# A 176-wide expert product without its zero padding: 48 rows in place of 128

## The reference

```python
def _L1_ffn_ref(hidden_states, gate_weight, w_gate, w_up, w_down):
    x = hidden_states.reshape(-1, H)              # 1024 tokens, H = 256
    scores = jax.nn.softmax(x @ gate_weight.T)    # E = 28 experts
    topk_w, topk_idx = jax.lax.top_k(scores, 6)
    topk_w = topk_w / (topk_w.sum(axis=-1, keepdims=True) + 1e-20)
    cw = ...                                      # 1024 x 28, zero but for the six
    def step(y, inp):
        wg, wu, wd, w_tok = inp                   # 256x176, 256x176, 176x256
        h = jax.nn.silu(x @ wg) * (x @ wu)
        return (y + w_tok[:, None] * (h @ wd), None)
```

## Time and profile before

| | us |
|---|---|
| median of 3 runs | 969.02 |
| the runs | 969.22, 964.23, 969.02 |
| profiled execution | 969.22 |
| its span, first to last instruction | 967.4 |
| mean granted TensorE clock | 0.828 |

### The profile page before, as it was taken

How to read it: one execution, slowest core, us unless ns; L and a number is a source line. 1 busy time by engine, 2 the same in 40 slices (tenths; PEclk the granted TensorE clock), 3 DMA queues, 4 the chain that set the end, 5 groups by cost and what they waited for, 6 DMA issues and landing times. The chain is left out here.

```text
span 967.4 us, 13065 instructions
## 1 busy us (share of the span) xinstructions
PE 733.1 (76%) x3998; PEld 503.0 (52%) x3998; DVE 583.8 (60%) x1541; ACT 295.5 (31%) x868; POOL 466.2 (48%) x395
## 2 busy tenths in 40 slices
PE   5889998888629785465586757887762799999991
PEld 3657776666416672133353434554441577777770
DVE  2457678796665629986787784353432255555554
ACT  2345555464200501011332323343420222222220
POOL 2146566675402103998639264014054266666662
PEclk9799999998858898657687767697855799999996
DMA  9999970002230010000000002192029466666657
GB/s 320 313 350 349 352 275 1 1 1 88 83 134 1 1 66 22 5 17 11 12 6 16 6 1 71 66 364 70 1 91 345 102 109 113 110 107 111 110 76 196
DMA packets 91169, 108.20 MB, mean 112 GB/s; under 512 B 21788, under 2 KB 83421, under 8 KB 90206
## 3 DMA queue, kind: packets, MB, share of 16 engines
q1 hardware_dynamic: 77276, 90.47, 28.6%
q0 software_dynamic: 13104, 16.52, 10.9%
q10 hardware_dynamic: 722, 0.37, 0.2%
HBM read 53.86 MB, written 53.49 MB: 111 GB/s over the span
## 5 line engine op out<-in xcount | busy, mean ns | idle before, releaser
L644 PE MATMUL PS<-W_all,fgu 128*128 x600 | 179.9, 423 | 0.2
L644 PE MATMUL PS<-R 128*64 128x256 f32 (+10 forms) x1004 | 158.3, 413 | 16.9 <-ACT R L2136 5.3
L1902 ACT ACTIVATE R<-PS 128x512 f32<-128x512 f32 (+5 forms) x183 | 88.7, 519 | 134.9 <-PE PS L644 70.3
L644 PEld LDWEIGHTS PS<-R 128*64 128x64 f32 (+3 forms) x1004 | 83.2, 173 | 78.0 <-issue 44.8
L652 PE MATMUL PS<-ident,R 128*128 128x128 f32 (+1 forms) x470 | 83.8, 324 | 46.0 <-ACT R L2136 21.7
L644 PEld LDWEIGHTS PS<-W_all,fgu 128*128 128x128 f32 x600 | 103.3, 192 | 21.8 <-issue 2.3
L2230 POOL TENSOR_SCALAR R<-R 128x256 f32<-128x256 f32 x88 | 80.9, 937 | 62.1 <-DVE R L1378 62.1
L652 PEld LDWEIGHTS PS<-ident,R 128*128 128x128 f32 (+1 forms) x470 | 62.4, 166 | 74.0 <-ACT R L2136 27.0
L2330 POOL DMA_INDIRECT y<-fwd,xh x45 | 69.7, 1549 | 54.5 <-DVE fwd L1869 53.9
L2297 POOL TENSOR_TENSOR R<-SelT,bqkv 128x2048 f32<-128x2048 f32 x16 | 61.4, 3856 | 46.3 <-DVE SelT L1680 46.0
L2219 POOL TENSOR_TENSOR rs<-rs,mh 128x1 f32<-128x1 f32 x48 | 27.1, 567 | 113.7 <-DVE rs L1278 113.4
(11 more groups left out here) (278 smaller groups left out, 1481.2 us busy)
## 6 DMA issues: line engine op xcount, KB each, us to landing
xg<-zrow SPq DMA_DIRECT2D x28, 1088.0 KB, 12.2
xh<-xg SPq DMA_DIRECT2D x45, 136.0 KB, 2.5
W_all<-in_wgu SPq DMA_DIRECT2D x1, 5760.0 KB, 16.9
W_all<-in_wgu SPq DMA_DIRECT2D x1, 5280.0 KB, 24.3
R<-in_wqkv SPq DMA_DIRECT2D x1, 4096.0 KB, 18.1
xT<-xg SPq DMA_DIRECT2D x30, 136.0 KB, 2.5
y<-zrow SPq DMA_DIRECT2D x3, 1152.0 KB, 11.8
yb<-y SPq DMA_DIRECT2D x3, 1024.0 KB, 6.5
```

Of the source, the lines that this page charges most:

```text
L644: return e.matmul(out, l, r, start=start, stop=stop, skip_group_check=True)
L1902: return e.activation(out, a, ACT.Copy)
```

## The change

The zero padding goes. `hm` becomes 176 wide, the second transpose takes its 48 last columns and writes 48 partitions, VectorE copies the two halves with an instruction each (128 and 48 partitions), and the second product of `ed` contracts over 48 partitions. Only 48 partitions of the last down weights are loaded; the zeros go from the array in HBM. The two memsets on GpSimd and VectorE's wait for them are removed.

```diff
-        hm = [cm(256) for _ in range(2)]
+        hm = [cm(176) for _ in range(2)]
...
-                e.dma_start(dst[:, :, 960:WE], D["wd2"][a:z].rearrange("e p n -> p e n")).then_inc(told, 16)
+                e.dma_start(dst[0:48, :, 960:WE], D["wd2"][a:z].rearrange("e p n -> p e n")).then_inc(told, 16)
...
-            def w_(j, off, n):
-                return W_all[:, bass.ds(at_w[j] + off, n)]
+            def w_(j, off, n, rows=128):
+                return W_all[0:rows, bass.ds(at_w[j] + off, n)]
...
                 tr(u.t[:, 0:128], hm[j % 2][:, 0:128])
-                tr(u.t[:, 128:256], hm[j % 2][:, 128:256]).then_inc(u.full, 1)
+                tr(u.t[0:48, 128:256], hm[j % 2][:, 128:176]).then_inc(u.full, 1)
...
                 mm(u.t[:, 0:256], hT_[j % 2][:, 0:128], w_(j, 704, 256), True, False)
-                mm(u.t[:, 0:256], hT_[j % 2][:, 128:256], w_(j, 960, 256), False, True).then_inc(u.full, 1)
+                mm(u.t[:, 0:256], hT_[j % 2][0:48, 128:256], w_(j, 960, 256, 48), False, True).then_inc(u.full, 1)
...
-                if j == 0:
-                    e.wait_ge(sem("hm0"), 2)
-                e.tensor_tensor(hm[j % 2][:, 0:176], u.t[:, 176:352], sg[j % 2], ALU.mult).then_inc(u.free, 1)
+                e.tensor_tensor(hm[j % 2], u.t[:, 176:352], sg[j % 2], ALU.mult).then_inc(u.free, 1)
...
-                e.tensor_copy(hT_[j % 2], u.t[:, 0:256]).then_inc(u.free, 1)
+                own.mark(e.tensor_copy(hT_[j % 2][:, 0:128], u.t[:, 0:128]))
+                e.tensor_copy(hT_[j % 2][0:48, 128:256], u.t[0:48, 128:256]).then_inc(u.free, 1)
...
-            def mp():
-                w = fill("xe_m", 3)
-                e.wait_ge(w.full, w.f + 1)
-                for i in range(2):
-                    e.memset(hm[i][:, 176:256], 0.0).then_inc(sem("hm0"), 1)
...
-    d["wd2"] = np.concatenate([wd[:, 128:176], np.zeros((NE, 80, 256), f)], 1)
+    d["wd2"] = wd[:, 128:176]
```

More of the change, by code:

```diff
@@ L2340, in _ @@
                     "l1_stat": lambda t0, t1: ln(range(t0, t1)), "l1_init": l1_init, "m2": m2, "m2s": m2s, "xp_stat": pair,
-                    "rt_stat": pair, "sc": sc, "mp": mp, "ed": ed}
+                    "rt_stat": pair, "sc": sc, "ed": ed}
             for name, args in P.seq:
```

## The result

The changed kernel takes 993.96 us (median of 4 runs, 992.37 to 999.83) against 969.12 for the kernel before (4 runs, 964.23 to 973.39): ratio 1.027, interval 1.021 to 1.033. It is slower by 2.7%, where 994.6 was forecast.

The account below looks back on a forecast made before the run. TensorE was taken to bound the expert loop at 2.488 us a block; 25.4 us of switches plus 0.14 for the copy made 25.5, and 969.22 + 25.5 = 994.7, stated as 994.6, range 978 to 1001.

Parts of the forecast that it names:

- The narrow transpose: Second transpose of `eh` with 48 stationary columns instead of 128: keeps its 0.109 us, so 0 change.
- The 48-row product: Second product of `ed` in each block: switching in and out costs emptying plus uncovered loads, 0.35 us a block.
- the first rival: At the `ed` switches only the emptying costs and loads stay hidden: 13.5 us more, time 983; chance 0.10.
- The fourth rival: `ed` product with register-addressed moving operand keeps the whole array, no switch: block 2.49 us, time 969.2; chance 0.11.
- The third rival: Pauses in the expert loop let TensorE's clock fall to its lower level: 1013 us and up; chance 0.03.
- The second copy: VectorE copying hT_ in two instructions: 0.14 us longer, hidden in the loop, coming through once at the end.
- Loads and memsets: Smaller loads of the weights' last 48 rows and removed GpSimd memsets, before the loop: all hidden, value 0.
- The end: Last scatters after the loop: the end moves by what block 72's scaling moves, 25.4 + 0.14 = 25.5 us.
- What would show it: Signs in the changed profile: 2.84 us block in the chain, `ed` as two shapes, late passes, TensorE less busy.

Follow-up runs that it names:

- all_but_rows: Changed kernel with the second product of `ed` back over 128 rows, narrow transpose and two copies kept: 985.68 us, ratio 0.999 to the kernel before.
- rows48_first: Changed kernel with the 48-row product of `ed` put before the 128-row one: 1010.06 us (kernel before, same chip: 987.87), block 2.878 us.
- rows48_cols65: Changed kernel with the 48-row product's stationary operand cut from 128 columns to 65: 1011.47 us (kernel before, same chip: 987.87), block 2.781 us.
- rows65_only: Kernel before with only the second product of `ed` cut to 65 rows: 987.26 us, ratio 1.001, block 2.493 us.
- rows64_only: Kernel before with only the second product of `ed` cut to 64 rows: 1006.68 us (kernel before, same chip: 987.87), block 2.833 us.

## Why the prediction was right

The forecast was 994.6, the median 993.96; the difference between the medians is 24.8 us against 25.5 forecast. That the medians come this near is in part luck, since the runs of either kernel lie 7 to 9 us apart; the firm comparison is the loop, 25.0 us longer in the profiles. Step by step:

- **The narrow transpose, 0.** Right; all_but_rows has it and a block of 2.489.
- **The 48-row product, 0.35 us a block.** Right in place and mechanism: 0.345 measured. Into the pair 0.093 and 0.104, out of it 0.091 and 0.057. That the load is a part of its own, which the forecast took from the length of a 64-row run, is shown by rows48_first and rows48_cols65; the first rival (emptying only, a block of 2.67) is out. Of the 0.09 the runs show the size and the place, in both directions and whatever is loaded next; that TensorE runs empty in it is the forecast's reading, and no run tests it. That the cost starts at 64 rows rested on a single step at the lower clock, between products of different operands; rows65_only and rows64_only show it with nothing else changed.
- **The register-addressed operand.** The fourth rival, to which 0.11 went, is out: a product whose streaming operand is addressed by a register switches like any other, at 64 and at 48 rows (2.833 us a block).
- **The clock.** 1.00 between 800 and 900 us in the traces of all twelve kernels. The third rival is out.
- **The second copy, 0.14 at the end.** Too dear: the two copies start 0.19 apart and the next instruction 0.20 after the second, 0.39 in all, where the next followed the one copy after 0.34. So 0.05. Against 25 us it changes nothing that can be measured.
- **Loads and memsets, 0.** Right. The last load lands 726.16 + 21.1 = 747.3, where the scatter lands at 755.6.
- **The end.** The scatter of block 72 waits for its scaling, and the last two follow at GpSimd's pitch, as said.
- **What would show it.** A block of 2.83 for 2.84, the pauses and their sizes came as listed. Three signs did not: the `ed` product stayed one row in the timeline, TensorE's busy share stayed at 100.00, and the chain of waits no longer runs through TensorE. All three come from how the profile is made, and whoever had looked there alone would have found no loss, or the wrong engine.

The Trainium skill's rule that a single product with small K takes as long as one with K = 128 ("TensorE: Matmul & The Clock Gate", "Why this matters for your kernels") holds here for a pass among its like (0.216 us inside a run of 64 rows as inside one of 128). It says nothing of the neighbours, and with it alone the change looks free. Its statement that a change of the tiling mode drains the engine ("TensorEngine Tiling (Array Packing)", "Key Properties") fits the 0.09 us of this trace. The 0.05 to 0.10 for the load behind it come on top and are about as large.

## What to carry to other kernels

Before cutting zeros from a contraction, look at what the rows next to it are: if it falls to 64 rows or fewer between products of more, each visit costs 0.35 us here (0.39 where the next pass is a product and not a transpose) and saves nothing: a pass took 0.109, 0.216 and 0.295 us with 128, 256 and 352 columns that stream, and 0.216 with 64 rows as with 128. That holds where TensorE sets the pace; where it waits for others, as in the cross-attention, nothing is won by avoiding it. Choose a split that keeps every part over 64 rows (88 + 88 rather than 128 + 48), or keep the padding. To find such costs, compare starts of consecutive passes and look for stationary loads that start together with their own pass; busy shares don't show them.

## What the runs showed of the hardware

- The step lies between 65 and 64 rows: 2.493 and 2.833 us a block for one row of zeros.
- A load that nothing covers costs by its columns: 65 in place of 128 took 0.053 us off a block (one trace).
- A float32 transpose with 48 stationary columns does not switch the array (block 2.489), where products with 17 columns start 0.09 late. No product with 48 stationary columns was run, so whether it is the transpose or the width that decides is open.
- The last load of the weights has 3/8 of its bytes and lands 21.1 us after its issue in place of 21.8. The load ahead of it, issued 0.4 us earlier, landed after 17.4 and 16.9 us. So the last one landed 4.1 us behind that one where it was 5.3: 3/8 of the bytes, on 48 partitions with rows of the same size, in some 3/4 of the time. That is one trace each, and nothing waited for it here.
